# Second attention: two-strip fp32r scores with DMA-laid heads in place of four-strip fp32 scores

## The chip, the cores and the metric

The kernel runs on one core of one Trainium2 chip. The metric is the device time of one execution in microseconds (us), lower being better.

## What is computed

A two-layer model on x of shape (4, 512, 256), with a context of the same shape. In order: a causal cross-attention with relative positions, a block with self-attention and a mixture of 8 experts (2 per token), a second cross-attention of 16 heads of 64, and a mixture of 16 experts (6 per token). The change touches the self-attention inside the second of these, called here the second attention, which has 16 heads of 16 in each of 4 batches:

```python
qkv = nx @ Wqkv + bqkv
q, k, v = jnp.split(qkv, 3, axis=-1)        # each (B, S, 16 heads, 16)
scores = jnp.einsum('bqhd,bkhd->bhqk', q, k) / jnp.sqrt(jnp.float32(HEAD_DIM))
scores = jnp.where(causal, scores, jnp.finfo(scores.dtype).min)
attn = jax.nn.softmax(scores, axis=-1)
out = jnp.einsum('bhqk,bkhd->bqhd', attn, v).reshape(B, S, D)
```

## The kernel before

Every engine has a program written out by hand, joined by semaphores; the order of instructions on each engine is the order of the code. The second attention (functions whose names end in `_f`, semaphores that begin with `f_`) works on NJ = 16 head groups of HQ = 4 heads, four groups for each batch of 512 tokens. A group is NUF = 8 steps, and each step handles two heads. For every head the scores are made twice:

- **Natural scores** (rows are queries) are only read for their row maximum. VectorE (DVE) adds the causal mask and takes the maximum in one instruction per head (`row_max`, L2101) and writes it into a column of `MX`.
- **Transposed scores** (rows are keys) go through exp on ScalarE (`exp_f`, L1686) into `PTf`. The maximum must already be subtracted by then. Before the change this is done by an extra row of the query operand: the maxima of a group are transposed by TensorE (`max_to_rows`, L1071) and added by DVE into `QP` (`queries_with_max`, L2106), where the keys `KP` have a constant -1 row (a bias of -1 from `bpad`).

In `scores_f(s)` TensorE issues for step s two matmuls of the transposed scores of group n (L1026) and two of the natural scores of a step AHEAD = 12 steps later (L1031), in turn. A head takes one 32-row strip of the array (16 rows of data and 16 masked ones), so the four matmuls lie in four strips and run side by side. All are fp32. The widths of both kinds over the 8 steps of a group are 512, 512, 384, 384, 256, 256, 128 and 128 columns, since the causal half is left out. The transposed scores use three PSUM banks (`STB`), two for each step: step s may begin once the first exp of step s-1 is done (`f_ex`). The natural ones use two double banks (`PD`).

Besides the scores TensorE has in a group: `values_f` at step 2 (16 matmuls of 17 columns of output for the group before, L1046), `out_to_tokens` at step 4 (4 transposes, L1077), `max_to_rows` at step 6, and, in some groups, projections of queries, keys and values (`queries_f`, `other_f`, all recorded at `project`, L806) and transposes of normalised tokens (L920). All of these write one PSUM bank, `MB`, in the order of the table `M_USES`; each waits until the use before it has been read. A projection of keys or queries serves eight heads, and ScalarE writes it out twice with masks, for even and odd heads (`keys_h` L1608, `queries_h` L1615). GpSimd (POOL) masks the diagonal blocks of `PTf` (L718) and, in groups 2 to 9, makes the residual (`residual_h`, L707 and L710).

The first attention (names ending in `_a`) runs just before. In its last turn (n = NJ) TensorE makes the first key and the first query projection of the second attention into free banks (`f_hw`, `f_hr`). After the second attention come its output projection, the routing and the experts. The weights of the output projection `WO` are loaded during the first attention.

The SyncE queue (SP) issues nearly all DMAs in program order; during the second attention it has none before the change.

Of the kernel before, what the change touches and what calls it, by code (L numbers as in the profile page):

```python
# [5 lines left out]
ALU = mybir.AluOpType  # L6
# [38 lines left out]
HQ = 4  # L45
# [6 lines left out]
Q_STEP, P_STEP, OT_STEP, MX_STEP = 0, 2, 4, 6  # L52
H_STEP1 = {0: ("hv", 0, 0), 1: ("hk", 1, 1), 3: ("hv", 1, 1), 5: ("hk", 2, 1), 7: ("hv", 2, 1), 9: ("hk", 3, 1),
           11: ("hv", 3, 1)}
H_STEP7 = {0: ("hk", 1, 0), 1: ("h", 6), 2: ("hv", 1, 0), 3: ("h", 7), 4: ("hk", 2, 0), 6: ("hv", 2, 0), 8: ("hk", 3, 0),
           10: ("hv", 3, 0)}
M_USES = [("hk", 0, 1), ("mx", 0)]
for _n in range(NJ + 1):
    M_USES += [("q", (_n + 2) // 2)] * (_n % 2 == 0 and _n + 2 < NJ)
    M_USES += [H_STEP1.get(_n)] * (_n in H_STEP1) + [("p", _n - 1)] * (_n >= 1) + [("hv", 0, 1)] * (_n == 0)  # L60
    M_USES += [("ot", _n - 1)] * (_n >= 1) + [("mx", _n + 1)] * (_n + 1 < NJ)
    M_USES += [H_STEP7.get(_n)] * (_n in H_STEP7)
M_AT = {use: i for i, use in enumerate(M_USES)}
M_W = {use: i for i, use in enumerate([_u for _u in M_USES if _u[0] != "p"])}
# [28 lines left out]
def head_of(g, j):  # L93

    return g // 2 * 2 * HQ + 2 * j + g % 2

# [106 lines left out]
def build(nc, A, out):  # L203

    with ExitStack() as ctx:
# [12 lines left out]
        def place(name, shape, dt, o=None):  # L218
            n = 1
            for s in shape[1:]:  # L220
# [34 lines left out]
        tmpA = [place(f"tmpA{i}", [P, RT, HQ * DH0], F32, rnrm + KB * i) for i in range(2)]  # L255
# [5 lines left out]
        WO = place("WO", [P, DK, D], F32, rQS + 2 * KB)  # L261
        KP = place("KP", [P, HGS, T], F32, rQB)
        QP = [place(f"QP{i}", [P, S], F32, rR1 + 2 * KB * i if i < 3 else rQS + 4 * KB) for i in range(4)]
        MX = [place(f"MX{i}", [P, RT, P], F32, rR1 + 6 * KB + 2 * KB * i) for i in range(2)]
        OS = [place(f"OS{i}", [P, S], F32, rR1 + 10 * KB + 2 * KB * i) for i in range(2)]
        rmask, rdump = region(2 * KB), region(2 * KB)
        maskw = place("maskw", [P, S], F32, rmask)
        PTf = [[place(f"PTf{i}_{c}", [P, HQ, S - c * P], F32, rPT + 20 * KB * i + KB * c * (9 - c)) for c in range(RT)]
               for i in range(2)]
        dump = [place("dump0", [P, S], F32, rdump), place("dump1", [P, S], F32, rnrm + 2 * KB)]  # L270
        nrmh = [place(f"nrmh{i}", [P, D], F32, o) for i, o in
                enumerate((rQB + 30 * KB, rQB + 31 * KB, rW0 + 4 * KB, rW0 + 5 * KB))]
# [103 lines left out]
        STB, MB = PS[4:7], PS[7]  # L376
# [10 lines left out]
              ("ctx0", "w0", "const", "x", "er", "wf", "wvo", "rows0", "late", "route", "ew", "wkq0", "wkq1", "wv1", "wo1", "x0", "x1", "wv0", "ctx1_0", "ctx1", "rows1", "we0", "we1", "we", "fc2b")}  # L387
# [29 lines left out]
        def t_done(eng, use):  # L417
# [4 lines left out]
        ln_sem = {t: {k: sem(f"ln{t}_{k}") for k in ("var", "sd", "nrm")} for t in range(5)}  # L422
# [14 lines left out]
        a_rc = sem("a_recip")  # L437
# [21 lines left out]
        f_rc = sem("f_recip")  # L459
        f_mw = sem("f_bank_written")  # L460
        f_mr = sem("f_bank_read")
# [7 lines left out]
        s_gate = sem("gates")  # L469
        s_e = {k: sem("moe0_" + k) for k in  # L470
               ("y", "x",
                "xt", "xT",
# [42 lines left out]
        def _(sp):  # L515
# [62 lines left out]
            sp.wait_ge(a_s, NJ * NUA)  # L578
# [9 lines left out]
            sp.wait_ge(f_mr, M_AT["ot", NJ - 1] + 1)  # L588
# [85 lines left out]
        def _(pool):  # L674
# [36 lines left out]

            pool.wait_ge(ld["rows0"], 48)
# [87 lines left out]
        def _(pe):  # L800
# [115 lines left out]
            def tokens_h(i):  # L916
                pe.wait_ge(ln_sem["h"]["nrm"], 2 * i + 2)
                for k in range(DK):
                    for x in range(2):
                        last = nc.tensor.transpose(MB[:, (2 * k + x) * P:(2 * k + x + 1) * P],  # L920
# [3 lines left out]
            def tokens_ha(i):  # L924
                bank_a(("h", i))
                tokens_h(i).then_inc(a_mw, 1)

            def keys_h(bank, b, half):
                return project(bank, lambda k: eight_heads(WFs[:, :, D:], k, half), lambda k: NT[:, k, b * S:b * S + S], S)

            def queries_h(bank, m):
                b, half = divmod(m, 2)
                return project(bank, lambda k: eight_heads(WFs, k, half), lambda k: NT[:, k, b * S:b * S + S], S)
# [33 lines left out]
            for n in range(NJ + 1):  # L967
                for u in range(NUA):
# [19 lines left out]
                    if n == NJ and u == 1:  # L988
# [3 lines left out]
                        keys_h(PS[0], 0, 0).then_inc(f_hw, 1)  # L992
                    if n == NJ and u == 2:
                        queries_h(PS[1], 0).then_inc(f_hw, 1)
# [4 lines left out]
            def bank_f(use):  # L999
                if M_AT[use]:  # L1000
                    pe.wait_ge(f_mr, M_AT[use])
                return MB

            def scores_f(s):
                n, u = divmod(s, NUF)
                c, pr = divmod(u, 2)
                g = s + AHEAD
                m, i = divmod(g, NUF)
                w = P * F_ROWS[i] + P
                if s >= 0:  # L1010
                    if u == 0:
                        pe.wait_ge(f_mr, M_AT["mx", n] + 1)
# [1667 lines left out]
```

## Time and profile before

| | |
|---|---|
| time, median of 3 runs | 1791.98 us (1789.44 to 1795.83) |
| span of the profiled execution | 1784.9 us |
| mean granted TensorE clock in it | 0.970 of 2.4 GHz |
| PE busy | 1648.8 us, 92% |
| DVE busy | 1082.9 us, 61% |
| ACT busy | 898.1 us, 50% |
| POOL busy | 352.6 us, 20% |
| first natural score of the second attention | 359.85 us from the span's start |
| first transposed score | 375.26 us |

The span is the time between the first and the last recorded instruction of one profiled execution. No run time of its own is given for that execution; the span lies 7.1 us under the median of the runs, and what lies around the span is taken as those 7.1 us. PE is TensorE, PEld its weight loads, ACT ScalarE, POOL GpSimd, SPq the DMA queue of SyncE. In rows of the timeline the first number is the start in us, the second the time that the row covers; "x4" says how many instructions it merges.

### The profile page before, as it was taken

The numbers are of one execution on the slowest core, as the hardware profiler recorded it, in microseconds if no ns is written. First come the engines' busy times: TensorE is split into PE (matmuls) and PEld (weight loads), VectorE is DVE, ScalarE is ACT, GpSimd is POOL, SyncE is SP. The second block draws the span as 40 slices with busy tenths as digits, with TensorE's granted clock in tenths as the row PEclk, the third lists the DMA queues.
The fourth block names the chain that finished last, engine by engine and source line by source line (L and its number), as shares of the span: only waits on it lengthen the run. The fifth ranks groups of instructions, "written<-read, shape, count | busy, mean of one in ns | idle before, by whom it ended". The sixth has DMA issues, their size and how long they took to land.

```text
span 1784.9 us, 32858 instructions
## 1 busy us (share of the span) xinstructions
PE 1648.8 (92%) x11314; PEld 1120.0 (63%) x11315; DVE 1082.9 (61%) x2944; ACT 898.1 (50%) x2088; POOL 352.6 (20%) x405
## 2 busy tenths in 40 slices
PE   8998989978888788999999799999999999989998
PEld 6555555533333386999999344566666566567887
DVE  4777677655556365222221687877776766767776
ACT  2888888635555422433334466665765765630000
POOL 1111111103432121111110421344232322110000
PEclk9999999889999887999999899999999999999999
DMA  8787778300000092111112311100010000020001
GB/s 304 260 284 258 275 256 292 118 1 1 1 1 1 10 382 79 38 36 35 38 36 68 111 50 31 59 19 25 24 30 24 19 25 18 13 83 1 1 0 47
DMA packets 74449, 149.64 MB, mean 84 GB/s; under 512 B 7024, under 2 KB 49648, under 8 KB 69840
## 3 DMA queue, kind: packets, MB, share of 16 engines
q1 hardware_dynamic: 70912, 138.64, 22.8%
q0 software_dynamic: 3408, 9.31, 1.8%
q8 instruction: 77, 1.26, 0.3%
q14 instruction: 52, 0.43, 0.1%
HBM read 96.68 MB, written 51.25 MB: 83 GB/s over the span
## 4 chain that ended last, share of the span: by engine, by line
PE 78%; DVE 9%; ACT 7%; issue 4%; DMA 1%; POOL 0%; SPq 0%; DVEq 0%; ACTq 0%; POOLq 0%
PE PS L1394 9%; PE PS L1231 8%; PE PS L1216 8%; PE PS L806 7%; PE PS L1349 6%; PE PS L1265 5%; PE PS L1364 5%; PE PS L1339 5%; PE PS L1026 5%; PE PS L873 4%; PE PS L895 3%; PE PS L1320 3%; PE PS L1046 2%; PE PS L906 2%; ACT PTf L1686 1%
## 5 line engine op out<-in xcount | busy, mean ns | idle before, releaser
L1813 ACT ACTIVATE P<-PS,nm 128x512 f32<-128x512 f32 x256 | 174.6, 694 | 108.4 <-DVE nm L2395 92.5
L1349 PEld LDWEIGHTS PS<-idf,P 128*128 128x128 f32 x1024 | 118.1, 143 | 98.8 <-issue 64.7
L2101 DVE CUSTOM_DVE_ANT_0 dump<-PS,maskw 128x256 f32<-128x256 f32 (+3 forms) x256 | 114.8, 487 | 92.3 <-PE PS L1031 87.1
L1349 PE MATMUL PS<-idf,P 128*128 128x128 f32 x1024 | 155.8, 282 | 12.4 <-ACT PTb L1823 11.0
L2012 DVE CUSTOM_DVE_ANT_0 SN<-PS,SR 128x128 f32<-128x128 f32 (+3 forms) x256 | 115.2, 487 | 83.8 <-PE PS L877 83.7
L2395 DVE TENSOR_REDUCE nm<-PS 128x2 f32<-128x1024 f32 x128 | 150.4, 1215 | 23.8 <-PE PS L1339 23.7
L1231 PEld LDWEIGHTS PS<-xT,W1c 128*128 128x128 f32 x1248 | 145.3, 192 | 4.2 <-ACT xT L1739 2.3
L1231 PE MATMUL PS<-xT,W1c 128*128 128x128 f32 x1248 | 145.8, 275 | 1.8 <-ACT xT L1739 1.8
L1026 PE MATMUL PS<-QP,KP 32*128 32x128 f32 (+3 forms) x512 | 107.6, 493 | 36.7 <-ACT PTf L1686 33.5
L1216 PE MATMUL PS<-EW,hT 128*128 x624 | 141.2, 379 | 0.0
L1686 ACT ACTIVATE PTf<-PS 128x512 f32<-128x512 f32 (+3 forms) x256 | 97.9, 435 | 82.7 <-PE PS L1026 82.6
L1565 ACT ACTIVATE SN<-SN,nm 128x128 f32<-128x128 f32 (+3 forms) x256 | 128.7, 555 | 7.2 <-DVE nm L2012 6.9
L1739 ACT ACTIVATE xT<-PS,cols 128x128 f32<-128x128 f32 x78 | 31.5, 454 | 197.0 <-PE PS L1206 197.0
L2286 DVE TENSOR_TENSOR ysb<-PS,fc2b 128x256 f32<-128x256 f32 x39 | 16.5, 424 | 187.3 <-PE PS L1216 187.3
L2615 DVE SCALAR_TENSOR_TENSOR X<-PS,gat,X 128x256 f32<-128x256 f32 x224 | 97.0, 479 | 46.2 <-PE PS L1394 45.3
L1216 PEld LDWEIGHTS PS<-EW,hT 128*128 128x128 f32 x624 | 115.6, 190 | 14.7 <-issue 0.4
L1364 PE MATMUL PS<-PTb,V 128*64 128x512 f32 x512 | 124.0, 605 | 0.0
L2404 DVE TENSOR_SCALAR P<-P,rc 128x512 f32<-128x512 f32 x256 | 121.1, 515 | 4.2
L873 PE MATMUL PS<-ErP,QPa 32*128 32x128 f32 (+3 forms) x448 | 91.2, 479 | 23.1 <-ACT EN L1558 14.0
L877 PE MATMUL PS<-Ka,QPa 32*128 32x512 f32 (+3 forms) x512 | 106.0, 488 | 2.7 <-DVE nm L2012 2.5
L1031 PE MATMUL PS<-KP,QP 32*128 32x384 f32 (+3 forms) x512 | 104.8, 492 | 4.0 <-DVE MX L2101 2.0
L895 PEld LDWEIGHTS PS<-idf,SN 128*128 128x128 f32 x640 | 68.5, 142 | 59.3 <-ACT SN L1565 35.1
(344 smaller groups left out, 3338.9 us busy)
## 6 DMA issues: line engine op xcount, KB each, us to landing
SR<-rel SPq DMA_DIRECT2D x16, 1024.0 KB, 8.0
rel<-EN SPq DMA_DIRECT2D x15, 1024.0 KB, 4.8
SR<-rel SPq DMA_DIRECT2D x16, 768.0 KB, 6.3
rel<-EN SPq DMA_DIRECT2D x15, 768.0 KB, 4.2
SR<-rel SPq DMA_DIRECT2D x16, 512.0 KB, 4.3
EW<-in_fc1T SPq DMA_DIRECT2D x8, 1024.0 KB, 11.8
EW<-in_fc2T SPq DMA_DIRECT2D x8, 1024.0 KB, 12.9
rel<-EN SPq DMA_DIRECT2D x15, 512.0 KB, 3.4
```

The lines of the kernel that those rows point to most:

```text
L806: last = mm(bank[0:m, 0:n], w(k), src(k), start=(k == 0), stop=(k == DK - 1))
L873: rel_mm = mm(PD[0][:, i, 0:w], QPa[e // 2 % 3][o:o + HQ8, r * P:r * P + P], ErP[e % 2][o:o + HQ8, S - w:S], start=True, stop=True)
L895: last = nc.tensor.transpose(TRA[i % 2][:, o:o + P], SN[(2 * t + j) % 6][:, c * P:c * P + P], idf[:])
L1026: keys_mm = mm(STB[(2 * s + x) % 3][:, 0:S - c * P], KP[o:o + HQ8, hg, b * S + c * P:b * S + c * P + P], QP[n % 4][o:o + HQ8, c * P:S], st ...
L1216: last = mm(PS[5][:, 0:D], hT[s][:, f, :], EW[:, bass.ds(e, 1), o:o + D].rearrange("p e d -> p (e d)"), start=(f == 0), stop=(f == FK - 1))
L1231: ins = mm(PS[1 + 2 * s + f // 4][:, f % 4 * P:f % 4 * P + P], W1c[s][:, o:o + P], xT[:, k, :], start=(k == 0), stop=(k == DK - 1), skip_g ...
L1349: last = nc.tensor.transpose(TR1[j][:, c * P:c * P + P], P1[s % 4][:, j, c * P:c * P + P], idf[:])
L1364: last = mm(OUT1[o:o + DH1, :], V1[chunk % NV1][:, m % VG, o:o + DH1], PT1[m % 2][:, j, c, :], start=(c == 0), stop=(c == RT - 1), skip_gr ...
L1394: last = mm(PS[tb % 8][:].rearrange("p (e n) -> p e n", e=2), x[:, k, t], w[i][:, :, k, :], start=(n + k == 0), stop=(n + k == len(parts) ...
L1565: af(sn, sn, ACT.Exp, bias=nm[:, (ku + i) % 16:(ku + i) % 16 + 1], scale=-1.0).then_inc(a_ex, 1)
L1813: last = af(P1[s % 4][:, j, :], PD[s % 2][:, j, :], ACT.Exp, bias=nm1[:, s % 4, j:j + 1], accum_out=sm1[:, s % 4, j:j + 1])
L2395: v.tensor_reduce(nm1[:, s % 4, :], PD[s % 2][:], AX.X, ALU.max, negate=True).then_inc(c_max, 1)
```

## The change

The heads of a group are now laid out by DMA. Each eight-head projection is written once as a high part (fp32r, by ScalarE, `high_h`) and once as the rest (fp32r, by DVE, `low_h`) into `HK` or `HQs`. SP then copies, for every group, 16-row pieces of these into strips of 64 rows: keys as high, high, low, and queries as high, low, high. Each strip's last 16 rows are filled once: -1 in two columns' rows of the key buffers `KD` (by GpSimd, `constant_rows`) and 0 in the query buffers `QD` (`zero_rows`). A strip pair holds four heads (`[P, 2, S]`). There are four key and three query buffers.

Natural scores are one fp32r matmul of 64 rows for each head. Transposed scores are two fp32r matmuls for each head into the same bank: keys by queries, then the same keys by `MS`, which holds the transposed maxima (high and rest) and zeros. DVE now writes the maxima to `mxs`, GpSimd places them with their rest in `MX` (`place_max`), TensorE transposes `MX` as before, and ScalarE copies the result to `MS` (`max_rows`); `queries_with_max` is gone. The single bank `MB` becomes two, used in turn, and natural scores use three single banks. Projections of the next batch are at odd steps; the keys and queries of the first batch (four projections instead of two) are made in the last turn of the first attention, and its values before the first natural score. `WO` is loaded at the end of the second attention. The head order of a group and of `ON` changes accordingly.

```diff
+            def strips(kind, m, rings, halves, parts):
+                b, g = divmod(m, HGS)
+                to = rings[m % len(rings)]
+                for x in range(2):
+                    rows = slice(DH0 * (HQ * x + g), DH0 * (HQ * x + g) + DH0)
+                    for i, part in enumerate(parts):
+                        o = HS * x + DH0 * i
+                        sp.dma_start(to[o:o + DH0].bitcast(F32), halves[rows, part].bitcast(F32))\
+                            .then_inc(f_ld[kind][m % len(rings)], 16)
+
+            def key_strips(m):
+                if m < HGS:
+                    sp.wait_ge(f_hr, 2)
+                elif m % HGS == 0:
+                    m_done(sp, ("hk", m // HGS, 1))
+                if m < NKD:
+                    sp.wait_ge(f_kc, (2, 5, 8, 11)[m])
+                else:
+                    sp.wait_ge(f_st, (m - NKD + 1) * NUF)
+                strips("k", m, KD, HK, (0, 0, 1))
...
+                    sp.wait_ge(f_st, (m - NQD + 1) * NUF)
+                strips("q", m, QD, HQs, (0, 1, 0))
+
+            key_strips(0)
+            for m in range(NJ):
+                query_strips(m)
+                if m + 1 < NJ:
+                    key_strips(m + 1)
+            sp.wait_ge(f_max, NJ * NSU)
             sp.dma_start(WO[:], A["wo"].rearrange("(k p) n -> p k n", p=P)).then_inc(ld["wvo"], 16)
...
+            def constant_rows(i):
+                for t in range(2):
+                    nc.gpsimd.tensor_scalar(KD[i][:, t], maskw[:], 0.0, kc[:, t:t + 1], ALU.mult, ALU.add).then_inc(f_kc, 1)
+
+            def zero_rows(i):
+                nc.gpsimd.memset(QD[i][:].bitcast(F32), 0.0).then_inc(f_kc, 1)
+
+            def place_max(n):
+                pool.wait_ge(f_max, n * NSU + NSU)
...
+            pool.wait_ge(s_bp, 3)
+            pool.wait_ge(a_tt, NJ * NSU)
+            constant_rows(0)
+            zero_rows(0)
+            constant_rows(1)
+            zero_rows(1)
+            pool.wait_ge(f_mz, 1)
+            pool.wait_ge(a_mr, len(A_USES))
+            pool.wait_ge(a_x, NJ)
+            constant_rows(2)
+            zero_rows(2)
+            constant_rows(3)
+            place_max(0)
             pool.wait_ge(ld["rows0"], 48)
             pool.wait_ge(a_mw, A_W["k", NJ // 2 - 1] + 1)
             for n in range(NJ):
                 for c in range(RT):
+                    if c == 2 and n + 1 < NJ:
+                        place_max(n + 1)
                     pool.wait_ge(f_ex, n * NSU + HQ * c + HQ)
...
                     if s >= 1:
                         pe.wait_ge(f_ex, 2 * s - 1)
+                    bank = lambda x: STB[(2 * s + x) % 3][:, 0:S - c * P]
+                    keys = lambda x: KD[n % NKD][HS * x:HS * x + HS, t, c * P:c * P + P]
+                    for x in range(2):
+                        mm(bank(x), keys(x), QD[n % NQD][HS * x:HS * x + HS, t, c * P:S], start=True, stop=False)
+                    for x in range(2):
+                        last = mm(bank(x), keys(x), MS[n % 2][HS * x:HS * x + HS, c * P:S], start=False, stop=True)
+                    last.then_inc(f_st, 1)
                 if m < NJ:
-                    if i == 0 and m // 2:
-                        pe.wait_ge(f_mr, M_AT["q", m // 2] + 1)
-                    if i == 0 and m % 2 == 0 and m:
-                        pe.wait_ge(f_mr, M_AT["hk", m // HGS, m % HGS // 2] + 1)
-                    if g >= 2:
-                        pe.wait_ge(f_max, 2 * g - 2)
-                for x in range(2):
-                    if s >= 0:
-                        b, hg = divmod(n, HGS)
-                        o = HQ8 * (2 * pr + x)
-                        keys_mm = mm(STB[(2 * s + x) % 3][:, 0:S - c * P], KP[o:o + HQ8, hg, b * S + c * P:b * S + c * P + P],
-                                     QP[n % 4][o:o + HQ8, c * P:S], start=True, stop=True)
...
+                    if i == 0:
+                        pe.wait_ge(f_ld["k"][m % NKD], 96 * (m // NKD + 1))
+                        pe.wait_ge(f_ld["q"][m % NQD], 96 * (m // NQD + 1))
+                    if g >= 1:
+                        pe.wait_ge(f_max, 2 * g - 1)
+                    for x in range(2):
+                        last = mm(NB[(2 * g + x) % 3][:, 0:w], QD[m % NQD][HS * x:HS * x + HS, y, r * P:r * P + P],
+                                  KD[m % NKD][HS * x:HS * x + HS, y, 0:w], start=True, stop=True)
+                    last.then_inc(f_nat, 1)
```

## Rows read from the trace of the kernel before

**Rows 1.** Second attention's loop: PE, PEld, DVE, ACT, POOL busy, PEclk, DMA, GB/s.

```profile
375.00:621.00 246.00, 202.18 (x1698) 88.08 (x1698) 132.49 (x536) 128.91 (x303) 70.59 (x95) 0.96 0.00 1
```

**Rows 2.** PE timeline, groups without projections: step 2, values, steps 4, 6, 0, 2.

```profile
583.50 0.58 PE L1026 MATMUL PS<-QP,KP 32*128 32x384 f32 x1 [0.70 <-ACT PTf L1686]
...
584.36 2.35 PE L1046 MATMUL PS<-PTf,VE 128*17 128x512 f32 x32
...
588.15 0.48 PE L1026 MATMUL PS<-QP,KP 32*128 32x256 f32 x1 [0.59 <-ACT PTf L1686]
...
590.59 0.37 PE L1026 MATMUL PS<-QP,KP 32*128 32x128 f32 x1 [0.49 <-ACT PTf L1686]
...
592.54 0.66 PE L1026 MATMUL PS<-QP,KP 32*128 32x512 f32 x1 [0.43 <-DVE QP L2106]
...
596.21 0.58 PE L1026 MATMUL PS<-QP,KP 32*128 32x384 f32 x1 [0.70 <-ACT PTf L1686]
```

**Rows 3.** ACT timeline of the same group, the two exps of a 512-wide step.

```profile
593.72 1.08 ACT L1686 ACTIVATE PTf<-PS 128x512 f32<-128x512 f32 x2 [1.11 <-PE PS L1026]
```

**Rows 4.** Chain that ended last: start us, us, what (two `values_f`, one projection).

```profile
404.20 2.35 PE PS L1046 x32
...
445.44 2.00 PE PS L806 x4
447.47 1.45 ACT QP L1615 x2
...
597.14 2.28 PE PS L1046 x32
```

**Rows 5.** Timeline at the start of the second attention (PE, POOL).

```profile
350.68 3.60 PE L806 MATMUL PS<-NT,WFs 128*128 128x512 f32 x8
...
359.85 1.24 PE L1031 MATMUL PS<-KP,QP 32*128 32x256 f32 x8 [1.89 <-DVE MX L2085]
...
375.26 1.19 PE L1026 MATMUL PS<-QP,KP 32*128 32x512 f32 x1 [0.52 <-DVE MX L2101]
...
358.79 0.73 POOL L695 TENSOR_TENSOR X<-X,tmpA 128x256 f32<-128x256 f32 x1 [8.71 <-DVE tmpA L2039]
```

**Rows 6.** Busy time in the last group (windows; the fraction 0.50 is the clock).

```profile
606.00:609.00 3.00, 2.31 (x8) 0.51 (x4) 0.00 (x0) 1.08 (x2) 0.00 (x0) 0.50 0.00 0
```

**Rows 7.** PE timeline in a later stage: fp32r scores of two 64-row strips.

```profile
1302.98 0.50 PE L1339 MATMUL PS<-KH,QH 64*128 64x512 f32 x2
1303.32 0.39 PE L1339 MATMUL PS<-KH,QL 64*128 64x512 f32 x2
1303.55 0.40 PE L1339 MATMUL PS<-KL,QH 64*128 64x512 f32 x2
```

**Rows 8.** DVE timeline of the same group: maxima added to the queries.

```profile
591.71 0.69 DVE L2106 TENSOR_TENSOR QP<-PS,QP 128x512 f32<-128x512 f32 x1
```

**Rows 9.** POOL groups by shape: count, busy us, mean ns of one.

```profile
L718 POOL TENSOR_SCALAR_AFFINE_SELECT PTf<-PTf 128x512 f32<-128x512 f32 x64 | 40.6, 635 | 190.5 <-ACT PTf L1686 190.5
...
L707 POOL TENSOR_SCALAR Hs<-X,mv,rsh 128x256 f32<-128x256 f32 x16 | 19.5, 1221 | 0.0
...
L676 POOL MEMSET ErP<- 128x512 f32 x2 | 1.0, 526 | 0.3 <-POOLq L2670 0.3
```

**Rows 10.** Eight 16-row DMAs: on the SP queue, and KB and us to landing.

```profile
2.78 3.70 SPq L525 DMA_DIRECT2D ErP<-in_ErT  x8
...
ErP<-in_ErT SPq DMA_DIRECT2D x8, 32.0 KB, 2.2
```

**Rows 11.** PE timeline of the last group, which has no natural scores.

```profile
605.23 1.91 PE L1026 MATMUL PS<-QP,KP 32*128 32x512 f32 x4 [0.47 <-ACT PTf L1686]
607.82 2.07 PE L1026 MATMUL PS<-QP,KP 32*128 32x512 f32 x4 [0.69 <-ACT PTf L1686]
...
612.17 4.07 PE L1046 MATMUL PS<-PTf,VE 128*17 128x512 f32 x32
...
621.36 2.35 PE L1046 MATMUL PS<-PTf,VE 128*17 128x512 f32 x32
```

More of the change, by code:

```diff
@@ L436, in build @@
         a_pv = sem("a_pv")
-        a_rc = sem("a_recip")
         a_mw = sem("a_bank_written")
@@ L924, in tokens_ha, with eight_heads_h @@
             def tokens_ha(i):
[L925 to L933, printed above, removed]
+                tokens_h(bank_a(("h", i)), i).then_inc(a_mw, 1)
+            def eight_heads_h(bank, kind, b, half):
+                w = WFs[:, :, D:] if kind == "hk" else WFs
+                return project(bank, lambda k: eight_heads(w, k, half), lambda k: NT[:, k, b * S:b * S + S], S)
             def keep_warm(count):
@@ L987, in _ @@
                         tokens_ha((n - 7) // 2)
-                    if n == NJ and u == 1:
+                    if n == NJ and u == 0:
                         pe.wait_ge(ld["wf"], 16)
@@ L1674, in other_f, with max_rows @@
                     return
-                act.wait_ge(f_mw, M_W[use] + 1)
-                last = tokens_h(use[1]) if use[0] == "h" else keys_h(MB, use[1], use[2])
-                last.then_inc(f_mr, 1)
+                bank = m_written(act, use)
+                if use[0] == "h":
+                    tokens_h(bank, use[1]).then_inc(m_read(use), 1)
+                else:
+                    kind, b, half = use
+                    if half == 0:
+                        for i in range(1, HGS):
+                            m, ring = HGS * (b - 1) + i, f_ld[kind[1]]
+                            act.wait_ge(ring[m % len(ring)], 96 * (m // len(ring) + 1))
+                        if kind == "hk":
+                            m = HGS * (b - 1)
+                            act.wait_ge(f_ld["k"][m % NKD], 96 * (m // NKD + 1))
+                    high_h(bank, kind, half)
+            def max_rows(n):
+                bank = m_written(act, ("mx", n))
+                if n >= 2:
+                    act.wait_ge(f_st, (n - 1) * NUF)
+                af(MS[n % 2][:], bank[:], ACT.Copy).then_inc(m_read(("mx", n)), 1)
             def exp_f(s):
@@ L2061, in normalise_h, with low_h @@
                         .then_inc(ln_sem["h"]["nrm"], 1)
+            def low_h(bank, kind, half):
+                to, c = (HK, COLS["bqkv"] + 2 + half) if kind == "hk" else (HQs, COLS["bqkv"] + half)
+                return v.scalar_tensor_tensor(to[:, 1, half], bank[:], cols[:, c:c + 1], to[:, 0, half].bitcast(F32), ALU.add,
+                                              ALU.subtract)
             for tb in range(RT):
@@ L2083, in _ @@
                         normalise_h((n - 6) // 2 + u - 6)
-            for i in range(2):
-                last = v.memset(MX[i][:], 0.0)
-            last.then_inc(f_mz, 1)
-            dve.wait_ge(f_mz, 1)
+                    if n == NJ and u == 4:
+                        v.memset(MX[:], 0.0).then_inc(f_mz, 1)
+                    if n == NJ and 1 <= u < 5:
+                        dve.wait_ge(f_hi, u)
+                        low_h(PS[u - 1], "hk" if u < 3 else "hq", (u - 1) % 2).then_inc(f_hr, 1)
             dve.wait_ge(s_causal, 2)
```

302 lines of the change are left out of this document (149 added, 153 removed).

## Prediction, made before the changed kernel was run

> **What bounds the kernel now.** The change touches only the second attention, so I read that stretch: its busy table, then the step starts of one bare head group, then the chain, for what the projections add. In the loop's 246 us [rows 1] PE is busy 202.2 us, DVE 132.5 and ACT 128.9. None is full; it is a loop of waits. A group without projections takes 596.21 - 583.50 = 12.71 us [rows 2]. In it two 512-wide steps take (596.21 - 592.54) / 2 = 1.84 us each. The step that starts at 592.54 has its first exp at 593.72 [rows 3]: 1.18 us from issue to exp. The exps take 1.08 us for two, and the next step may start once the first is done, since three banks serve two heads. So a 512-wide step is 1.18 us of PE latency plus 0.65 us of exp and hand-over, and PE idles at the end of it. The 384-wide step before `values_f` is bound by PE instead: 0.86 us of scores from 583.50 to 584.36, then values, recorded as 2.35 us [rows 2].
>
> From 404.20 to 597.14 there are 13 groups [rows 4]: 192.9 us, 27.7 us more than 13 x 12.71. In them lie 16 projections and two transposes of tokens (0.6 us each, a guess from the four transposes of the other uses), so a projection adds (27.7 - 1.2) / 16 = 1.65 us: about 2.00 us of PE and, for keys and queries, 1.45 us of ACT after it [rows 4], partly in gaps. The whole loop, 375.26 [rows 5] to 621.36 (the last values) [rows 11], is then 16 x 12.71 + 21 x 1.65 + 1.2 = 239.2 us, and the 6.9 us left over are mostly the half clock of its first and last groups [rows 6].
>
> **The scores.** fp32 cost now: 512 columns in four strips, two recorded instructions each, 1.18 us to the exp. After: two fp32r passes on two strips. [Rows 7] show exactly this: pair starts 0.34 and 0.23 us apart, so a 512-wide pair costs 0.23 us of PE, and the second ends about 0.39 us after its start. Latency 0.34 + 0.39 + 0.08 of hand-over = 0.81 us, a gain of 0.37 us in each of two steps. The gain scales with columns: 0.28 us for the 384-wide step bound by the exp, 0.18 for each 256-wide one of (590.59 - 588.15) / 2 = 1.22 us [rows 2]. The step before `values_f` gains only on PE: 0.86 to about 0.62, 0.24 us. At the group's end I count nothing: today maxima are transposed and DVE adds them in 0.69 us [rows 8]; after, ACT copies them (one 512-wide ACT operation, about 0.54 us, half of [rows 3]) ahead of its last two exps, and the next group waits for both. Sum: 0.74 + 0.28 + 0.36 + 0.24 = 1.62, so 11.1 us for a bare group, 16 x 1.62 = 26 us. The natural matmuls follow the transposed ones and leave the loop; DVE, 132.5 us of 246, stays below the new length.
>
> The trace has no fp32r matmul narrower than 512 columns here. Bounds: cost by columns, as taken (from the nearest row, the 512-wide one), or, above, no better than fp32, four times the column time. Four times 256 columns at 2.4 GHz are 0.43 us a pair, so a 256-wide step takes PE 1.28 us, with the transposes of one of them (0.6) 1.9 against 1.22 now; a 128-wide one 0.64, with its transposes 1.24 against about 1.0. With the lost 0.36 that is some 1.6 us a group, which eats the 26 us.
>
> **Projections.** 18 remain in the loop against 21: the last two of batch 0's keys and queries move to the end of the first attention, and its values before the first natural score. ACT's share falls from 1.45 to one 0.6 us copy, DVE gets 0.69 us for the low part in slack. I take 1.45 us each (PE's 2.00 less a gap of about 0.55): 26.1 us against 34.7. Two M banks take waits away; counted at nothing beyond this, the gaps hide them.
>
> **POOL.** `place_max` stands behind POOL's mask (0.64 us) and, in groups 2 to 9, a residual of 1.22 + 0.73 = 1.95 us [rows 5, 9]. The masks' exps end 1.6 us into step 3; the placed maxima come about 4.9 us into it, and PE wants them 3.7 us after it begins (a step of 1.23, two of 1.05, the scores of step 6). Where no projection lies between, in groups 3, 4, 7 and 8, PE waits about 1.3 us: +5.2 us. Queued behind the waiting transposes are step 7 and the next group.
>
> **The strips.** 12 DMAs a group on SP's queue. Eight 16-row DMAs take 3.70 us to issue, 0.46 each, and land in 2.2 [rows 10]: 5.6 us of queue in an 11.1 us group. Queries go first: issued once the group three before is done, last landed 6 x 0.46 + 2.2 = 5.0 us later, wanted after steps 0 to 3 with the values, about 7.5 us. Hidden, by 2.5 us; late next would be PE at step 4. Nothing else is on SP here; `WO` comes behind the last strips, 12 steps before it is wanted, at no cost. The strips of [rows 10] have half the bytes of the new ones, from HBM and not SBUF: bound below 0.46 us each, above a whole landing, 2.2 us each, not overlapped; I take the lower, as issue overlaps landing in that row. The Trainium skill (SBUF — State Buffer, "Door 1: The DMA port swizzle") says that 16 neighbouring partitions reach only 4 of 16 ports, measured 104 GB/s. By it a 64 KB strip would hold its ports 0.63 us, and the queries would land after 6.0 us, an estimate from that page; still hidden, with less margin. No row here shows that limit.
>
> **The start.** Today natural scores start at 359.85 and transposed ones at 375.26 [rows 5]. After: two more projections in the last turn, 3.60 us for two [rows 5], move the end of the first attention; POOL's last add, at 358.79 for 0.73, then ends at 363.1. Only then does POOL reach `constant_rows`: 128x512 with two operations. Bounds: 0.64 us (the mask, 128x512) and 2.44 (twice L707's 128x256) [rows 9]; I take 2.44, the same operation. Two give 368.0, 12 strips take until 373.5, landed 375.7: first natural score. Meanwhile POOL makes the other six constant rows and three zero buffers (2 x 0.53 each): 363.1 + 8 x 2.44 + 3 x 1.05 = 385.8, then places the maxima (0.6), PE transposes and ACT copies (about 1.9 at 1.2 GHz): first transposed score at 388.3, 13.0 us later. With the low price natural scores start at 372 and 12 steps of about 1 us give 384. The projections moved out of the loop have no cover here: they and the strips behind them are in these 13 us.
>
> **Sum.** 16 x 11.1 + 18 x 1.45 + 1.2 + 5.2 + 5.0 (half clock at the ends, shorter passes) = 215.1 us from 388.3: end at 603.4 against 621.36, 18.0 us earlier. What follows moves with it. The profiled execution, 1784.9 us of span with 7.1 around it, is the median run; 1792.0 - 18.0 = **1774 us**.
>
> **Rivals.**
> - **Clock (slower).** The last group, with natural scores gone, fills two of four strips and the clock falls to 0.50, 1.2 GHz [rows 6]; a 512-wide step then takes 607.82 - 605.23 = 2.59 us against 1.84, and values 4.07 against 2.35 [rows 2, 11]. After, the strips are full but columns stream 0.64 us of a 1.46 us step, against 0.85 of 1.84: about as dense, thinner in the narrow steps. At half clock a group would take about 5 us more (2.6 for the scores, 1.8 for values, the rest transposes), 80 us in all: 1774 + 80 = 1854 at worst. From 23% of the loop at 1.2 GHz it is slower than before. Against it: 0.96 over the whole of today's loop [rows 1]. Chance 0.08.
> - **Strips bound the group (slower).** From 11.1 / 12 = 0.93 us a strip the queue sets the pace; at 1.2 us, 14.4 us a group, +53: 1827. Against it, the 0.46 us of [rows 10]. Chance 0.03.
> - **Narrow fp32r costs like fp32.** At both narrow widths the 26 us are gone, 1774 + 26 = 1800 (slower, chance 0.03). At 128 columns alone it costs (1.24 - 1.0) x 16 = 4 us, still in the forecast.
> - **The scores are not what limits a step.** If exp, maxima and their hand-overs give back half of the 26 us, 1774 + 13 = 1787, no change that can be told. DVE's adding or ACT's copying of the maxima at a group's end speaks for it, the PE latency of 1.18 us against it [rows 2, 3]. Chance 0.11.
> - **Better than taken.** Constant rows at the low price (4 us), projections wholly in gaps (0.4 us each, 7), POOL never late (5), warm ends: 1774 - 16 = 1758. The idle PE in [rows 2] speaks for some of it. Chance 0.19.
>
> **Numbers.** The forecast, 1766 to 1783, has 0.56. Range 1757 to 1797: it holds the forecast, most of the better case and the no-change case. A change of 0.3% (5.4 us) is what a measurement can tell: faster 0.56 + 0.19 = 0.75, same 0.11, slower 0.08 + 0.03 + 0.03 = 0.14.
>
> **What would show it.** Right: 512-wide steps at 1.4 to 1.5 us and a bare group at 11 us; strips landing before step 4, no PE idle put down to a DMA; first transposed score near 388 with POOL's constant rows ahead; DVE in the loop under 75%. Wrong: a granted clock under 1 in mid-loop; fp32r matmuls of 128 columns longer than 0.3 us; PE waiting on `KD`, `QD` or `MS` for more than a microsecond a group; a stage longer than today's 262 us (359.85 to 621.4).

## The result: no gain, 0.24% slower

The changed kernel takes 1796.52 us (median of 20 runs, 1789.9 to 1802.0), the kernel before 1791.05 (20 runs, 1786.93 to 1795.83). The ratio is 1.0024, interval [1.0015, 1.0032]. It is slower clear of the noise, by 5.5 us between the medians; by the ratio that is less than the 0.3% that I called no change. A gain of 18 us was forecast. The range of 1757 to 1797 holds the result by half a microsecond, which is luck.

### The profile page after: what moved, and what is told of

Its sections match the earlier page's. It is cut to its first block, busy times and chain, and to the rows that moved or that the text cites. A ratio compares the mean times of both kernels' runs of the same rounds, so it can differ in the third digit from the quotient of the medians.

```text
span 1795.4 us, 32572 instructions
## 1 busy us (share of the span) xinstructions
PE 1665.4 (93%) x11058; PEld 1151.3 (64%) x11059; DVE 1084.7 (60%) x2945; ACT 892.7 (50%) x2088; POOL 368.0 (20%) x448
## 4 chain that ended last, share of the span: by engine, by line
PE 77%; DVE 8%; ACT 7%; issue 5%; POOL 1%; DMA 1%; SPq 0%; DVEq 0%; ACTq 0%; POOLq 0%
PE PS L1479 9%; PE PS L1316 8%; PE PS L1301 8%; PE PS L912 7%; PE PS L1434 6%; PE PS L1350 5%; PE PS L1449 5%; PE PS L1424 5%; PE PS L979 4%; PE PS L1001 3%; PE PS L1405 3%; PE PS L1140 3%; PE PS L1116 2%; PE PS L1012 2%; ACT PTf L1769 1%
## 5 line engine op out<-in xcount | busy, mean ns | idle before, releaser
L1434 PE MATMUL PS<-idf,P 128*128 128x128 f32 x1024 | 155.7, 282 | 12.0 <-ACT PTb L1904 10.5
L1001 PE MATMUL PS<-idf,SN 128*128 128x128 f32 x640 | 98.9, 286 | 1.5 <-DVE PTa L2111 1.4
L1904 ACT ACTIVATE PTb<-PS 128x512 f32<-128x512 f32 x128 | 76.9, 600 | 34.1 <-PE PS L1434 34.0
```

What stands on the lines that cost most here:

```text
L1001: last = nc.tensor.transpose(TRA[i % 2][:, o:o + P], SN[(2 * t + j) % 6][:, c * P:c * P + P], idf[:])
L1434: last = nc.tensor.transpose(TR1[j][:, c * P:c * P + P], P1[s % 4][:, j, c * P:c * P + P], idf[:])
```

## The profile after

First the loop, from the first transposed score to the last step of scores, as the windows view gives it (columns: window, its length, busy us and instructions of PE, PEld, DVE, ACT and POOL, granted clock, DMA share, GB/s). It answers to [rows 1].

```profile
388.10:626.70 238.60, 208.86 (x1448) 111.46 (x1446) 129.92 (x529) 124.91 (x304) 77.70 (x125) 0.85 0.28 46
```

It starts at 388.1, as forecast. Up to the last values, which start 0.6 us behind this window at 627.29, it takes 239.2 us where 215.1 were forecast and 246.1 before. ("Loop" of a run below is the window up to the last step, 238.6 us here.) The granted clock is 0.85 against 0.96 before. 0.85 is a mean of two levels, 1.00 and 0.50: in 0.15 x 2 x 238.6 = 72 us of the loop the clock was 1.2 GHz, before in 0.04 x 2 x 246 = 20 us.

Three stretches of 20 us in mid-loop, kernel before:

```profile
448.00:468.00 20.00, 15.98 (x140) 6.20 (x136) 10.74 (x43) 12.16 (x27) 7.00 (x9) 1.00 0.00 1
508.00:528.00 20.00, 15.97 (x133) 6.29 (x136) 10.60 (x42) 12.29 (x27) 7.00 (x9) 1.00 0.00 1
568.00:588.00 20.00, 15.71 (x162) 5.98 (x160) 11.32 (x46) 11.00 (x25) 3.17 (x5) 1.00 0.00 1
```

And the changed kernel:

```profile
448.00:468.00 20.00, 16.96 (x106) 9.33 (x107) 9.39 (x46) 8.70 (x24) 9.99 (x16) 0.69 0.28 46
508.00:528.00 20.00, 16.27 (x118) 8.96 (x117) 10.90 (x54) 9.73 (x27) 10.59 (x17) 0.81 0.26 43
568.00:588.00 20.00, 17.34 (x122) 9.90 (x120) 11.70 (x55) 10.57 (x29) 4.71 (x10) 0.74 0.29 48
```

PE's busy share is higher than before in all three, and the clock is lower: the same work takes longer at the lower level, so the share alone doesn't tell the clock. Now one of these places in the timeline of PE (start, time covered, idle time before and its releaser):

```profile
511.10 0.63 PE L1161 MATMUL PS<-idf,MX 128*128 128x128 f32 x4 [0.75 <-POOL MX L801]
511.66 0.33 PE L1116 MATMUL PS<-QD,KD 64*128 64x128 f32 x2
511.82 0.28 PE L1118 MATMUL PS<-MS,KD 64*128 64x128 f32 x2
511.94 0.28 PE L1127 MATMUL PS<-KD,QD 64*128 64x128 f32 x2
512.68 0.51 PE L1116 MATMUL PS<-QD,KD 64*128 64x512 f32 x2 [0.46 <-ACT PTf L1769]
...
514.10 0.79 PE L1116 MATMUL PS<-QD,KD 64*128 64x512 f32 x2 [0.39 <-ACT PTf L1769]
514.70 0.63 PE L1118 MATMUL PS<-MS,KD 64*128 64x512 f32 x2
515.12 0.63 PE L1127 MATMUL PS<-KD,QD 64*128 64x512 f32 x2
516.02 0.69 PE L1116 MATMUL PS<-QD,KD 64*128 64x384 f32 x2 [0.27 <-ACT PTf L1769]
```

PE waits 0.75 us for POOL's placed maxima, and some 3 us later the same instruction takes 0.79 us instead of 0.51. The step from 512.68 takes 1.42 us, the one from 514.10 takes 1.92. Why POOL is late shows in its timeline, here in the first of the four groups with this wait:

```profile
446.65 1.22 POOL L782 TENSOR_SCALAR Hs<-X,mv,rsh 128x256 f32<-128x256 f32 x1
447.95 0.72 POOL L785 TENSOR_TENSOR Hs<-Hs,rows 128x256 f32<-128x256 f32 x1
448.65 0.26 POOL L799 TENSOR_SCALAR MX<-mxs 128x16 fp32r<-128x16 f32 x1
449.00 0.23 POOL L801 TENSOR_TENSOR MX<-mxs,MX 128x16 f32<-128x16 f32 x1
```

The residual (the first two rows) stands ahead of `place_max` (the other two) on POOL. The start of the stage, PE's timeline:

```profile
361.13 0.66 PE L1019 MATMUL PS<-idf,OSa 128*128 128x128 f32 x4 [0.71 <-ACT OSa L1671]
362.80 5.38 PE L912 MATMUL PS<-WFv,NT 128*128 128x256 f32 x16 [1.01 <-DVE tmpA L2122]
374.30 0.58 PE L1127 MATMUL PS<-KD,QD 64*128 64x256 f32 x2 [6.12 <-DMA QD<-HQs]
...
378.26 0.80 PE L1127 MATMUL PS<-KD,QD 64*128 64x512 f32 x2 [0.40 <-DVE mxs L2190]
379.85 0.80 PE L1127 MATMUL PS<-KD,QD 64*128 64x512 f32 x2 [0.80 <-DVE mxs L2190]
...
388.05 0.74 PE L1116 MATMUL PS<-QD,KD 64*128 64x512 f32 x2
```

POOL's and SP's queues in it:

```profile
362.62 0.73 POOL L770 TENSOR_TENSOR X<-X,tmpA 128x256 f32<-128x256 f32 x1 [12.47 <-DVE tmpA L2122]
363.34 1.37 POOL L789 TENSOR_SCALAR KD<-maskw,kc 128x512 fp32r<-128x512 f32 x2
364.65 0.95 POOL L792 MEMSET QD<- 128x1024 f32 x1
...
364.78 3.77 SPq L623 DMA_DIRECT2D KD<-HK  x6
368.66 3.70 SPq L623 DMA_DIRECT2D QD<-HQs  x6
```

Natural scores wait 6.12 us for the strips, which wait for POOL's constants, which stand behind its last addition. The 12 natural steps then run at 1.2 GHz.

The end of the stage is slower too. From the last values to the first matmul with `WO` it is 9.3 us (627.29 to 636.58), at a granted clock of 0.51, against 5.4 us before (621.36 to 626.78), at 1.00. The last values, 2.35 us before [rows 11], take in PE's timeline:

```profile
627.29 4.47 PE L1140 MATMUL PS<-PTf,VE 128*17 128x512 f32 x32
```

## The experiments

Two theories stood against each other. **Clock**: the loop is thin enough for TensorE's clock to fall at small waits, and what is lost at 1.2 GHz takes back the gain. **Rivals**: the strips' DMAs, the late maxima by the length of their wait alone, or the start. Edits are to the changed kernel unless said otherwise; ratios are to the kernel before. The changed kernel stands at 1.0024.

**e1, no strips.** After the first fill of each buffer no strip is copied, so later groups compute on the first groups' heads; that part of the work is left out. That is 150 of 192 copies, not the 110 of the expectation. The waits for later copies are lowered to match (not shown).

```diff
-            for m in range(NJ):
+            for m in range(NQD):
                 query_strips(m)
-                if m + 1 < NJ:
+                if m + 1 < NKD:
```

> The changed kernel without the strip DMAs after the first of each buffer (4 key and 3 query groups are laid, the others reuse what lies there); it leaves out 110 of about 192 strip copies or more, so the scores of later groups are of the wrong heads. In the changed kernel the granted clock over the loop (389.9 to 632.5 us) is 0.84 against 0.96 before, and 1.0024 of the time of before. Theory A (the lost clock is the loss): nothing changes, loop clock 0.82 to 0.86, ratio 1.000 to 1.004. Rival B (the strips' transfers, 0.63 us each on the queue, hold up TensorE or disturb something): loop shorter by 5 us or more, ratio under 0.999.

1.002 [1.0005, 1.0035], no different from the changed kernel. Strips in the loop cost nothing that can be told, though DMA is busy 28% of it with them and 2% without. The granted clock of the loop stays low, 0.87.

**e2, natural scores twice**, so only added work.

```diff
-                    for x in range(2):
+                    for x in (0, 1, 0, 1):
                         last = mm(NB[(2 * g + x) % 3][:, 0:w], QD[m % NQD][HS * x:HS * x + HS, y, r * P:r * P + P],
                                   KD[m % NKD][HS * x:HS * x + HS, y, 0:w], start=True, stop=True)
```

> The changed kernel with every natural matmul pair issued twice before its semaphore: TensorE has 128 more pairs of 53 to 213 ns at full clock, 17 us of added work, in the gaps in which it waits for the exp. Theory A (clock): the granted clock over the loop rises from 0.84 to 0.93 or more and the time falls in spite of the added work, by 8 to 20 us, ratio 0.991 to 0.998. Rival C (the lost time is TensorE's own work and waits): loop clock may rise or not, the time rises by 2 to 17 us, ratio 1.003 to 1.012.

1.0008 [0.9997, 1.0019]. The loop, where one more pair a step is issued:

```profile
396.30:629.00 232.70, 210.55 (x1678) 119.36 (x1677) 130.34 (x529) 124.69 (x304) 77.75 (x125) 0.96 0.27 46
```

232.7 us at 0.96 against 238.6 at 0.85, with 230 more matmuls in it. But the loop starts 8.2 us later in this profile, and the ratio is only 0.0016 (2.9 us) lower, with intervals that overlap. Both forecasts missed: the clock came back, and the added work took nearly all that it gave.

**e3, maxima placed first.** The first of POOL's two residuals in a group moves from behind the second mask, ahead of `place_max`, to behind the third; the other stays behind the fourth.

```diff
-                    if n >= 2 and c % 2 == 1 and 2 * n - 4 + c // 2 < TB:
-                        residual_h(2 * n - 4 + c // 2)
+                    if n >= 2 and c >= 2 and 2 * n - 4 + c - 2 < TB:
+                        residual_h(2 * n - 4 + c - 2)
```

> The changed kernel with GpSimd's residual work moved from behind the second mask of a group to behind the third, so that placing the maxima is never behind it. It takes away a wait of 0.75 us of TensorE for GpSimd in 4 groups, after which the clock was seen to fall. If GpSimd's wait is only its own price: 3 to 4 us less, ratio about 1.000, loop clock still 0.84. If that wait is what makes the clock fall (a form of theory A): loop clock 0.90 or more and 10 us or more less, ratio 0.993 to 0.998.

0.9937 [0.9919, 0.9956]: 15.6 us under the changed kernel, for four waits of 0.75 us, 3.0 us in all in the table of waits. Its loop takes 228.2 us at 0.89. More than the waits came back, as the form of the clock theory said.

**e4, value projections spread**: from steps 1 and 3 of the third group of a batch to steps 1 and 5 of the fourth.

```diff
-(4 * _b + 2, 1): ("hv", _b + 1, 0), (4 * _b + 2, 3): ("hv", _b + 1, 1)
+(4 * _b + 3, 1): ("hv", _b + 1, 0), (4 * _b + 3, 5): ("hv", _b + 1, 1)
```

> The changed kernel with the value projections moved from the third group of a batch (steps 1 and 3) to the fourth (steps 1 and 5), which has none today; the work is the same. Theory A with the bare groups as the place where the clock falls: the clock stays up in more of them, loop clock 0.88 or more, 5 us or more less, ratio 0.995 to 1.000. If only the amount of work counts and not where it lies: ratio 1.002 +- 0.002, loop clock 0.84.

0.9977 [0.9962, 0.9992]. The same work in another order gives 8 us; the loop is 229.1 us at 0.90.

**e5, one pass.** The transposed scores' second pass, which subtracts the maxima, is left out.

```diff
                     for x in range(2):
-                        mm(bank(x), keys(x), QD[n % NQD][HS * x:HS * x + HS, t, c * P:S], start=True, stop=False)
-                    for x in range(2):
-                        last = mm(bank(x), keys(x), MS[n % 2][HS * x:HS * x + HS, c * P:S], start=False, stop=True)
+                        last = mm(bank(x), keys(x), QD[n % NQD][HS * x:HS * x + HS, t, c * P:S], start=True, stop=True)
```

> The changed kernel without the second transposed pass; it leaves out the subtraction of the maxima (they are still found, placed, transposed and copied). By the latency of a step alone this takes 0.24 us off each 512-wide step, less in narrow ones, about 1.1 us a group: 15 to 18 us, ratio 0.992 to 0.994. Theory A (clock): TensorE has 17 us less columns to stream, the granted clock over the loop falls from 0.85 to 0.80 or less, and what the shorter latency gives is lost again: ratio 0.998 to 1.006.

1.0046 [1.003, 1.0062]: **no faster than the changed kernel, with 256 matmuls less** (by the ratios 4 us slower, though the intervals just touch), where the shorter steps alone were expected to give 15 us or more. Its loop takes 237.8 us at a clock of 0.80. Two windows of it in mid-loop, clock 0.70 and 0.75:

```profile
448.00:468.00 20.00, 16.31 (x112) 7.99 (x104) 10.62 (x47) 9.99 (x27) 8.91 (x13) 0.70 0.34 56
508.00:528.00 20.00, 16.40 (x116) 7.20 (x108) 9.91 (x43) 9.13 (x24) 7.48 (x12) 0.75 0.37 60
```

The clock isn't all of it: PE's waits for DVE's maxima in the loop rise from 3.9 to 11.0 us, so part of the shorter step is lost to DVE. How the two share the loss wasn't separated.

**e6, e3 and e4 together.**

> Both orders changed, as in e3_place_first (0.9937 of the time of before) and e4_spread (0.9977), with no work added. Theory A: loop clock 0.92 or more (e3 0.89, e4 0.90), loop about 222 us against 228 and 229, ratio 0.988 to 0.992. If the two cured the same falls of the clock: ratio 0.993 to 0.995, clock 0.90.

0.9946 [0.9927, 0.9964], not to be told from e3, as if the two edits cured the same falls; its loop takes 222.7 us at 0.92. From 585.2 to 596.8 the clock is 1.00, and a group without projections can be read off between two starts of `values_f`:

```profile
585.21 2.35 PE L1140 MATMUL PS<-PTf,VE 128*17 128x512 f32 x32
596.78 2.35 PE L1140 MATMUL PS<-PTf,VE 128*17 128x512 f32 x32
```

11.57 us, against 12.71 before [rows 2].

**e7, filled**: e6 with the natural pair twice within the loop and pairs without a reader where no natural scores are left. **e8, warm**: e7 with 12 matmuls ahead of the first natural score.

```diff
-                    for x in range(2):
+                    for x in ((0, 1, 0, 1) if s >= 0 else (0, 1)):
```

> e6_place_spread, with the natural matmul pair issued twice once the loop runs, and one pair without a reader in the steps that have no natural scores left. Added work, to hold the clock. Theory A: loop clock 0.97 or more; e2_nat_twice (the same filling) got 6 us from it at a clock of 0.96 against 0.85, but here less clock is lost to begin with: ratio 0.985 to 0.992, within 4 us of e6_place_spread either way. Rival C (added work is only added work): 5 to 15 us more than e6_place_spread.

> e7_filled with 12 small fp32 matmuls without a reader before the first natural score, in the 6 us in which TensorE waits for the first strips at 1.2 GHz. The 12 steps ahead of the loop then run at 2.4 GHz: theory A says 2 to 3 us less than e7_filled. If those steps are bound by VectorE and hand-overs: no difference.

e7: 1.0009 [0.9995, 1.0024], e8: 1.0003 [0.9989, 1.0016]. The clock of e7's loop is 0.98, but the filling is not free: the groups' starts at 579.23 and 591.71 are 12.48 us apart, 0.91 more than in e6, or 14.6 us over 16 groups. By the ratios e7 takes 0.0063 of 1791, 11.3 us, more than e6, as its rival said: once the order is mended, filling every step costs more than the clock gives back. e8's matmuls bring nothing that can be told.

**e9, constants early**: e6 with POOL's constant rows of the first two buffers ahead of its last addition of the first attention; the same lines are gone from their old place (not shown).

```diff
+                if n == NJ + 1:
+                    pool.wait_ge(s_bp, 3)
+                    pool.wait_ge(a_tt, NJ * NSU)
+                    constant_rows(0)
+                    zero_rows(0)
+                    constant_rows(1)
+                    zero_rows(1)
```

> POOL lays the constant rows and zero rows of the first two buffers ahead of its last addition of the first attention, on top of the order of e6_place_spread (place_max first, the hidden units' projections spread). If POOL's constants are what the strips of the first group wait for, the first natural score comes some 6 us earlier (366 to 368 instead of 372 to 378) and the ratio to the kernel before is 0.991 [0.989 to 0.993]. Rival: the strips wait for the projected heads or the DMA queue, and the ratio stays at e6's 0.9946 with the first natural score within 1 us. A third outcome: the start is earlier, but the loop runs longer at a lower granted clock, and half or more of the 6 us are lost again.

0.9903 [0.9886, 0.9919]. PE's timeline:

```profile
363.84 0.66 PE L1020 MATMUL PS<-idf,OSa 128*128 128x128 f32 x4 [0.72 <-ACT OSa L1672]
365.51 5.38 PE L913 MATMUL PS<-WFv,NT 128*128 128x256 f32 x16 [1.01 <-DVE tmpA L2123]
370.82 0.39 PE L1128 MATMUL PS<-KD,QD 64*128 64x256 f32 x2
```

From the last transposes of the first attention to the first natural score it is 6.98 us, in e6 13.18 (366.64 to 379.82): 6.2 us less, without a wait. The start I gave for the first score, 366 to 368, was missed, because those transposes themselves start between 361 and 367 us in the profiled executions.

**e10, early and warm**: e9 with five matmuls in PE's wait for the last normalised rows. **e12, start filled**: e10 with one to three matmuls behind each natural pair of the 12 steps ahead.

```diff
+            for _ in range(5):
+                mm(PS[0][:, 0:P], idf[:], idf[:], start=True, stop=True)
             pe.wait_ge(a_mr, len(A_USES))
```

```diff
                     last.then_inc(f_nat, 1)
+                    if s < 0:
+                        for _ in range((1, 2, 3, 3)[F_ROWS[i]]):
+                            mm(STB[0][:, 0:P], idf[:], idf[:], start=True, stop=True)
```

> e9_early with five more fp32 matmuls into the projections' accumulator ahead of PE's wait for the last normalized rows, so that PE is busy in that wait. Clock theory: the two rows of hidden-unit projections and the 12 natural steps of the first group run at 2.4 GHz instead of 1.2; 3 to 8 us less than e9_early. Rival: PE isn't the limit in this stretch, and the time is e9's or up to 2 us above it.

> e10_early_warm with one to three extra fp32 matmuls (128x128, results overwritten) behind each pair of natural scores in the 12 steps before the first transposed ones, where PE waits 0.4 to 0.8 us a step for DVE's maxima. Clock theory: these steps, and the first group behind them, run at 2.4 GHz instead of 1.2 from step 6 on: 2 to 5 us less than e10_early_warm, ratio 0.984 to 0.986. Rival: DVE's maxima set these steps whatever the clock, and the loop's clock falls by itself a little later; the ratio stays within 0.001 of e10_early_warm's 0.987.

e10: 0.9871 [0.9848, 0.9894], e12: 0.9869 [0.9855, 0.9884]. In e10 the value projections take 3.62 us instead of 5.38, but then the clock falls. The windows of e10 and then of e12:

```profile
375.00:385.00 10.00, 6.61 (x26) 3.86 (x28) 6.96 (x31) 1.68 (x3) 0.48 (x2) 0.50 0.63 103
385.00:395.00 10.00, 8.78 (x47) 5.68 (x43) 7.52 (x35) 5.71 (x14) 2.35 (x5) 0.50 0.17 29
```

```profile
375.00:385.00 10.00, 9.54 (x64) 6.91 (x64) 7.89 (x35) 1.68 (x3) 0.48 (x2) 1.00 0.64 104
385.00:395.00 10.00, 7.87 (x46) 4.61 (x43) 7.99 (x38) 7.70 (x17) 2.36 (x5) 0.80 0.34 57
```

The filling lifts the clock where it was meant to, 0.50 to 1.00 and 0.80, and the profiled loop is 217.9 us against e10's 224.6. The ratios are equal within their intervals, which is what the rival said, and e9's and e10's intervals overlap too: what either filling is worth by itself stays open. e12's interval lies just under e9's, so the two together gain something. e12 at 1767.30 us (1767.17 to 1768.32) against 1791.2 is with e10 the best version, 1.3% faster than the kernel before and 1.5% than the change.

**e11, filled wait.** The experiment that decides. Nothing is moved or removed; in the four groups with the 0.75 us wait, PE gets three more matmuls ahead of it.

```diff
                 bank = m_bank(("mx", n))
+                if n in (4, 5, 8, 9):
+                    for _ in range(3):
+                        mm(bank[:, 0:P], idf[:], idf[:], start=True, stop=True)
                 pe.wait_ge(f_mx, n + 1)
```

> The changed kernel as it is, with three extra fp32 matmuls (128x128, results overwritten) on PE ahead of its wait for the placed maxima, only in the four groups in which the changed kernel's PE waits 0.75 us for POOL there. Nothing is removed and no wait is made shorter; the three fit into the wait. Clock theory: PE stays busy, the clock does not fall there, the four groups come 1.5 to 3 us shorter each, and the time is 5 to 10 us below the changed kernel's (ratio to the kernel before 0.997 to 0.9995). Rival, that the late maxima cost by the wait itself and what is queued behind it: the time is the changed kernel's, 1.0024, or up to 1 us more.

0.9969 [0.9951, 0.9987], 1787.41 us: twelve matmuls more make the kernel 9.8 us faster by the ratio (0.0055 of 1791). The place in the timeline, and the three stretches from above:

```profile
512.65 0.94 PE L1161 MATMUL PS<-idf 128*128 128x128 f32 x6
513.43 0.62 PE L1164 MATMUL PS<-idf,MX 128*128 128x128 f32 x4
513.97 0.33 PE L1116 MATMUL PS<-QD,KD 64*128 64x128 f32 x2
```

```profile
448.00:468.00 20.00, 16.63 (x162) 9.81 (x160) 12.98 (x55) 11.91 (x30) 10.04 (x15) 1.00 0.43 70
508.00:528.00 20.00, 17.07 (x157) 10.98 (x150) 11.85 (x56) 11.23 (x30) 11.10 (x17) 1.00 0.34 56
568.00:588.00 20.00, 16.11 (x152) 9.18 (x154) 13.81 (x62) 12.23 (x31) 5.03 (x10) 1.00 0.38 63
```

The maxima come as late as before (in this group POOL ends them 1.38 us after PE begins step 6, in the changed kernel 1.37), but the clock holds 1.00 in all three, where it had 0.69, 0.81 and 0.74. It isn't 1.00 everywhere: from 428 to 448 us it is 0.83, where the changed kernel's profile has 1.00, and from 588 to 608 it is 0.74 in both. So the whole loop is the better measure:

```profile
392.50:621.10 228.60, 200.31 (x1472) 111.42 (x1472) 129.76 (x529) 124.84 (x304) 77.99 (x125) 0.91 0.29 48
```

0.09 x 2 x 228.6 = 41 us at 1.2 GHz instead of 72, and 10.0 us less, which is what the ratio says. The other runs agree, each with its mean granted clock: the changed kernel's 20 go from 1789.90 us at 0.956 to 1802.00 at 0.947, e11's 12 from 1777.48 at 0.964 to 1792.15 at 0.955, and at 0.956 both kernels take 1787 to 1790 us. So the clock costs the gain, shown for 9.8 us of it by an edit that takes no work and no wait away. That the rest is the clock's too is reckoned below and not shown by an edit, and what makes it fall in the groups that were not filled was not tested.

## Why the prediction was wrong

**The step that failed is the one about the clock.** The sum charged half clock only at the loop's two ends (the 5.0 us), and the Clock rival had a chance of 0.08. It is what happened. In it, "At half clock a group would take about 5 us more" and "from 23% of the loop at 1.2 GHz it is slower than before" were near: the loop had 72 of 238.6 us there, 30%, and the kernel is just slower. The argument against it, "0.96 over the whole of today's loop", did not carry over. I compared how densely columns stream in a 512-wide step and called it "about as dense". After the first group the clock fell nine times. Once it was in a group with projections, near 418 us, behind a wait of 1.22 us for DVE's maxima. The other eight were at the end of a group with no projection in steps 0 to 6 or at the start of the next: four at, or up to 2.3 us behind, the four waits of 0.75 us (near 449, 466, 513 and 527 us), and four near 571, 589, 602 and 616, at no such wait. The kernel before holds 1.00 from 508 to 528 us through waits of 0.96, as its PE timeline shows:

```profile
510.12 0.58 PE L1026 MATMUL PS<-QP,KP 32*128 32x384 f32 x1 [0.96 <-ACT PTf L1686]
```

So the length of one wait doesn't decide; what does, these runs don't show.

**The size.** From the sum of 215.1 us to 239.2 are 24.1. The bare group is 11.57 at full clock and not 11.1, 16 x 0.47 = 7.5 us. POOL's waits were 3.0 and not 5.2, -2.2. The remaining 18.8 are put down to the clock as what is left over. With the 5.0 already counted for half clock at the ends they are 24 us for 72 us at 1.2 GHz, about a third of a microsecond each. Two other readings give about the same: e11's loop (10.0 us for 31) and the changed kernel's own runs (12.1 us for a clock of 0.947 instead of 0.956, that is 32 us more at 1.2 GHz). Behind the start of the last values the span has 1168.1 us left against 1163.5 before, where I let what follows move along unchanged; 3.9 of these 4.6 us are the slower end of the stage. The profiled executions overstate the loss, 10.5 us of span against 5.5 by medians. I took the profiled execution of the kernel before for its median run, 7.1 us above its span; in all its runs that have both numbers the span lies only 1.7 to 1.8 us under the time, so it was one of the quicker ones, near 1786.6 us. My 18.0 us taken from that would have given 1769 and not 1774.

**The scores: right.** Two 512-wide steps at full clock in the changed kernel's timeline of PE, and the exps of the first in that of ACT:

```profile
500.31 0.50 PE L1116 MATMUL PS<-QD,KD 64*128 64x512 f32 x2 [0.47 <-ACT PTf L1769]
500.62 0.42 PE L1118 MATMUL PS<-MS,KD 64*128 64x512 f32 x2
...
501.73 0.50 PE L1116 MATMUL PS<-QD,KD 64*128 64x512 f32 x2 [0.45 <-ACT PTf L1769]
```

```profile
501.08 1.09 ACT L1769 ACTIVATE PTf<-PS 128x512 f32<-128x512 f32 x2 [0.75 <-PE PS L1118]
```

The step takes 501.73 - 500.31 = 1.42 us against 1.46, and 0.77 us from issue to exp against 0.81. The group's end is where I counted nothing for ACT's copy of the maxima; the bare group's extra 0.47 us may lie there, which wasn't tried alone. **Narrow fp32r: half right.** Pairs of 128 columns start 0.11 to 0.17 us apart at full clock, between the 0.06 of "cost by columns", which I took, and the 0.21 of the upper bound. Pairs of 256 start 0.12 to 0.22 apart, near the 0.12 taken and far from 0.43. My mark for it, a duration over 0.3 us, was reached (0.28 to 0.33 us in the rows above), but badly chosen: such durations overlap.

**The projections: right.** Four groups of e12 with six projections, from the start of `values_f` at 474.34 to the one at 529.63, take 55.3 us, four bare ones 4 x 11.57 = 46.3. So a projection adds 9.0 / 6 = 1.50 us, against 1.45.

**POOL: right in place, half right in size, wrong in price.** 0.75 us each in four groups against 1.3; but "queued behind the waiting transposes are step 7 and the next group" left out the clock. Of the 15.6 us that e3 gains, at most 3.0 are the waits.

**Strips: right that they are hidden, wrong value taken.** Six take 3.77 us to issue, 0.63 each, not 0.46, and land in 2.3. My row, strips half as big from HBM, was the worse guide. The estimate from the Trainium skill (SBUF — State Buffer, "Door 1: The DMA port swizzle") was 0.63 us a strip; the trace agrees with it, as the queue takes 0.63 us for each. e1 shows no cost of the strips in the loop. In the start 12 x 0.17 = 2 us of them have no cover.

**The start: right by errors that cancel, and by luck.** First natural score 374.30 (forecast 375.7), first transposed 388.05 (388.3). But `constant_rows` costs 0.69 us an instruction, near my low bound of 0.64, and not the 2.44 that I took from another operation with two operands read by pointer (twice L707 of the kernel before); POOL is done at 371.4 and waits 13 us for the maxima. What fills the time instead are the slower strips, the value projections (5.38 us at 1.2 GHz) and 12 steps at 1.2 GHz. And this profile is the earliest of all: in e1 to e7 and e11, with the same code up to there, the first natural score starts at 378.5 to 379.9, and where the steps ahead are as in the changed kernel the first transposed one at 392.2 to 393.7.

**The marks.** Of those for "wrong" two came true: the 0.3 us of the narrow matmuls, which meant little, and the granted clock in mid-loop, which told the cause. The stage's length, set at 262 us, did not: it ran from 374.3 to 627.3, 253 us, but began 14.5 us later, so that mark could not see the loss. The better case had its early POOL part in e3 and its start in e9. With both repaired and the clock held in more of it, e12's loop takes 217.9 us at 0.95, near the 215.1 of the sum, and its 1767 us lies below my 1774. So the shorter steps can carry the gain that was forecast, but in that number the start repaired in e9 has its part.

## What to carry to other kernels

Where TensorE waits on other engines at every step, taking work off it can lower its clock, and the loss comes back as longer steps everywhere: read the granted clock in windows of mid-loop before and after, not the busy share. First take away short waits that recur (an engine's order, here POOL's residual before the maxima), then put a few idle matmuls into the waits that remain, and only there, since filling inside the steps cost as much as it gave or more (e2, e7). Price a wait by the clock it can cost as well as by its length.

## What was not expected of the hardware

- Removing 256 matmuls made the kernel no faster (1.0046 against 1.0024), adding 12 made it faster (0.9969).
- Once the three matmuls filled the four waits, the clock held also in the 568 to 588 us window, where nothing had been filled; it still fell near 422, 429, 593 and 610 us. Why it does there stays open.
- The execution before the second attention varies: the last transposes of the first attention start at 361.13 in the profile of the changed kernel and at 366.64 in e6, whose code is the same up to there. The granted clock is 1.00 from 150 to 180 us and from 240 to 270 in the first and 0.94 in the second, so the clock falls there in some executions only. A difference of some 5 us in the start of a stage between two profiles says nothing by itself.
- The `tensor_scalar` of `constant_rows`, with one constant and one operand read by pointer, takes POOL 0.69 us for 128x512 (L789); that of the residual, with two operands read by pointer, takes 1.22 us for 128x256 (L782).
